# Second attention of a two-layer kernel: scores built from differences of key tiles, a PSUM bank of its own for projected queries, the row maximum transposed later

## The reference, cut to what matters

```python
# second attention: 16 query heads of width 128, 8 key/value heads, 1601 context rows
q = (text_hidden @ Wq).reshape(B, T_text, N_HEADS, HEAD_DIM).transpose(0, 2, 1, 3)
k = (vision_tokens @ Wk).reshape(B, T_vis, N_KV_HEADS, HEAD_DIM).transpose(0, 2, 1, 3)
v = (vision_tokens @ Wv).reshape(B, T_vis, N_KV_HEADS, HEAD_DIM).transpose(0, 2, 1, 3)
scores = jnp.einsum('bhtd,bhsd->bhts', q, k) / scale
scores = jnp.where(mask, scores, -jnp.inf)
attn = jax.nn.softmax(scores, axis=-1)
out = jnp.einsum('bhts,bhsd->bhtd', attn, v)
return out.transpose(0, 2, 1, 3).reshape(B, T_text, N_HEADS * HEAD_DIM) @ Wo
```

## Time and profile before

| | |
|---|---|
| median of 3 runs | 1723.7 us (1720.66 to 1727.66) |
| profiled execution, its own time | 1719.67 us |
| its span, first to last instruction | 1718.4 us |
| mean granted TensorE clock | 0.953 |
| busy: PE, DVE, ACT, POOL | 1520.5, 1257.4, 1056.7, 756.7 us |

### The profile page before, as it was taken

One profiled execution on the slowest core, in us unless ns is written; L12 is line 12 of the kernel. 1 busy time (PEld: TensorE's weight loads), 2 busy tenths in 40 slices (PEclk: granted clock), 3 DMA queues, 4 the chain that ended last, 5 costly groups with the idle time before them and its releaser, 6 DMA issues.

```text
span 1718.4 us, 25847 instructions
## 1 busy us (share of the span) xinstructions
PE 1520.5 (88%) x8715; PEld 747.0 (43%) x8812; DVE 1257.4 (73%) x2460; ACT 1056.7 (61%) x1755; POOL 756.7 (44%) x573
## 2 busy tenths in 40 slices
PE   5787988888878799699999999989999999999989
PEld 3243343343223442234444544444545556455445
DVE  6765766666785346488898789999678886888946
ACT  3567668568657355267766566756457665666734
POOL 3014024024020011166787567676476665566733
PEclk8798999999989799789999999999999999999999
DMA  4001101101120310100001000010000000000000
GB/s 151 1 1 44 36 2 26 34 1 24 37 80 2 161 38 1 29 20 1 20 20 31 1 1 26 1 30 2 1 1 1 1 1 1 1 1 1 1 1 25
DMA packets 20490, 36.72 MB, mean 21 GB/s; under 512 B 4898, under 2 KB 15238, under 8 KB 19334
## 3 DMA queue, kind: packets, MB, share of 16 engines
q1 hardware_dynamic: 20358, 35.07, 7.1%
HBM read 26.53 MB, written 1.15 MB: 16 GB/s over the span
## 4 chain that ended last, share of the span: by engine, by line
PE 43%; DVE 7%; issue 6%; ACT 3%; POOL 1%; DMA 0%; DVEq 0%; POOLq 0%; ACTq 0%
PE BK L510 43%; DVE arena L1678 4%; DVE arena L1701 2%; ACT arena L1780 1%; POOL arena L1817 1%; ACT arena L1784 1%; DVE arena L1670 0%; ACT L1780 0%; ACT L762 0%; PE BK L1601 0%; PE BK L778 0%; DVE arena L1687 0%; ACT arena L1770 0%; DVE arena L1684 0%; DVEq L446 0%
## 5 line engine op out<-in xcount | busy, mean ns | idle before, releaser
L510 PE MATMUL BK<-arena 128*128 128x512 bf16 (+11 forms) x8385 | 1473.7, 374 | 139.3 <-DVE arena L1678 25.1
L510 PEld LDWEIGHTS BK<-arena 128*128 128x128 bf16 (+5 forms) x8482 | 711.5, 114 | 869.3 <-issue 237.2
L1817 POOL TENSOR_TENSOR arena<-arena 128x512 f32<-128x512 f32 (+1 forms) x352 | 504.7, 1434 | 226.8 <-ACT arena L1780 208.7
L1701 DVE TENSOR_TENSOR arena<-arena 128x512 bf16<-128x512 f32 (+1 forms) x416 | 430.3, 1038 | 23.4 <-ACT arena L1784 22.1
L1780 ACT ACTIVATE arena<-BK,arena 128x512 f32<-128x512 f32 (+1 forms) x416 | 285.6, 687 | 255.0 <-PE BK L510 254.5
L1034 DVE TENSOR_REDUCE arena<-BK 128x1 f32<-128x512 f32 x384 | 243.7, 683 | 60.2 <-PE BK L510 59.3
L1678 DVE CUSTOM_DVE_ANT_0 arena<-BK,arena 128x512 bf16<-128x512 f32 x384 | 262.5, 684 | 23.1 <-PE BK L510 5.9
L1184 ACT ACTIVATE arena<-BK 128x512 f32<-128x512 f32 (+1 forms) x416 | 226.0, 598 | 67.2 <-PE BK L510 60.3
L1784 ACT CAST arena<-arena 128x512 bf16<-128x512 f32 (+1 forms) x416 | 257.1, 618 | 13.2
L1224 POOL TENSOR_TENSOR arena<-arena 128x256 f32<-128x256 f32 (+6 forms) x45 | 30.2, 671 | 208.9 <-ACT arena L1123 206.6
L1814 POOL TENSOR_TENSOR arena<-arena 128x512 f32<-128x512 f32 x32 | 45.5, 1422 | 88.7 <-ACT arena L1780 88.7
(11 more groups left out here) (157 smaller groups left out, 825.0 us busy)
## 6 DMA issues: line engine op xcount, KB each, us to landing
arena<-arena SPq DMA_DIRECT2D x144, 50.0 KB, 2.2
arena<-in_ctxT SPq DMA_DIRECT2D x8, 800.5 KB, 5.4
arena<-in_ctxk SPq DMA_DIRECT2D x4, 768.0 KB
arena<-in_wqT SPq DMA_DIRECT2D x1, 2048.0 KB, 8.9
arena<-in_wo SPq DMA_DIRECT2D x1, 2048.0 KB, 13.3
arena<-in_x SPq DMA_DIRECT2D x4, 256.0 KB, 11.3
arena<-in_rsel SPq DMA_DIRECT2D x1, 1024.0 KB, 9.4
arena<-in_rw1T SPq DMA_DIRECT2D x1, 1024.0 KB, 5.1
```

The lines of the kernel that those rows point to most:

```text
L510: return T.matmul(out_, lhsT, rhs, start=start, stop=stop, skip_group_check=True)
L1701: V.tensor_tensor(Pl[k][0:m, :], P1[k][0:m, :], Ph[k][0:m, :], ALU.subtract).then_inc(p_low, 1)
L1817: G.tensor_tensor(acc[0:m, g % 2, :], acc[0:m, g % 2, :], P1[k][0:m, :], ALU.add).then_inc(summed1, 1)
```

## The change

For key tiles 2 to 12 `s1` no longer starts the bank anew. It adds the product of queries with the difference between this tile's keys and those of two tiles earlier, which lie in the same bank; the maximum is already in it. So the fourth matmul is there for tiles 0 and 1 alone. The differences and their bf16 halves (`dch`, and `ctl` from column 256) are formed in stage 1, in `cx`, which now starts at step 12. The projected queries get bank 6, `ql` becomes a piece that comes a tile later on DVE, `o1a` and `o1b` move to bank 7, `o1a` multiplies by one column of ones instead of 128, `m1n` comes a half tile later, and `pace` draws 20 steps for each 26 half tiles.

```diff
@@ stage1: context() is drawn from step 12 on
-            next(cside, None)
+            if s >= E - 4:
+                next(cside, None)
@@ stage2
         def qproj(g):
-            piece("qp", g, bank=7)
-            yield
+            piece("qp", g, bank=6)
+            yield
+            yield
+            piece("ql", g)
             yield
@@ finish
-            piece("o1a", g, bank=6)
+            piece("o1a", g, bank=7)
             yield
             yield
-            piece("o1b", g, bank=6)
+            piece("o1b", g, bank=7)
@@ pace
-            while paced[0] * 26 < (2 * (s + LEAD1) + half) * 18:
+            while paced[0] * 26 < (2 * (s + LEAD1) + half) * 20:
@@ buffers
+        dch = [sb(f"dch{b}", [128, S2 - 256], BF16, L1) for b in range(3)] + [sb("dch3", [128, S2 - 256], BF16, MN)]
-        qa = sb("qa", [128, 1024], F32, L1)
-        qb_ = sb("qb_", [128, 1024], F32, L1)
+        qa = sb("qa", [128, 1024], BF16, L1)
+        qb_ = sb("qb_", [128, 1024], BF16, L1)
@@ vector_moe, cx
                     V.tensor_copy(cth[:, b, :], ctf[b % 2]).then_inc(ct_high, 1)
+                    dve.wait_ge(ct_done, 2 * b + 1)
+                    V.tensor_tensor(ctf[b % 2][:, 0:S2 - 256], ctf[b % 2][:, 256:S2], ctf[b % 2][:, 0:S2 - 256],
+                                    ALU.subtract).then_inc(ct_step, 1)
+                    dve.wait_ge(ct_step, b + 1)
+                    dve.wait_ge(*emptied("fold", H - 1))
+                    V.tensor_copy(dch[b][:, :], ctf[b % 2][:, 0:S2 - 256]).then_inc(ct_step_high, 1)
@@ gpsimd_moe, cx
-                    G.tensor_tensor(ctl[:, b, :], ctf[b % 2], cth[:, b, :], ALU.subtract).then_inc(ct_done, 1)
+                    G.tensor_tensor(ctl[:, b, 0:256], ctf[b % 2][:, 0:256], cth[:, b, 0:256], ALU.subtract).then_inc(ct_done, 1)
+                    pool.wait_ge(ct_step_high, b + 1)
+                    G.tensor_tensor(ctl[:, b, 256:S2], ctf[b % 2][:, 0:S2 - 256], dch[b][:, :],
+                                    ALU.subtract).then_inc(ct_done, 1)
@@ tensor_l1, s1
+                    high = cth[:, b, ks] if kt < 2 else dch[b][:, 128 * kt - 256:128 * kt - 256 + m]
-                    mm(o, cth[:, b, ks], qh[:, r, :], stop=False)
-                    mm(o, cth[:, b, ks], ql[:, r, :], start=False, stop=False)
-                    mm(o, ctl[:, b, ks], qh[:, r, :], start=False, stop=False)
-                    pe.wait_ge(rows1[g % 2], 16 * (g // 2 + 1))
-                    mm(o, onb[:, 0:m], mrw[:, g % 2, :], start=False).then_inc(full[i], 1)
+                    if kt < 2:
+                        pe.wait_ge(rows1[g % 2], 16 * (g // 2 + 1))
+                        mm(o, onb[:, 0:m], mrw[:, g % 2, :], stop=False)
+                    mm(o, high, qh[:, r, :], start=False, stop=False)
+                    mm(o, high, ql[:, r, :], start=False, stop=False)
+                    mm(o, ctl[:, b, ks], qh[:, r, :], start=False).then_inc(full[i], 1)
@@ tensor_l1, o1a
-                        t = mm(BK[6][:, 128 * u:128 * u + 128], acc[:, g % 2, 128 * u:128 * u + 128], ones[:, :])
+                        t = mm(BK[7][:, u:u + 1], acc[:, g % 2, 128 * u:128 * u + 128], ones[:, 0:1])
```

More of the change, by code:

```diff
@@ L610, in program @@
         ckl = sb("ckl", [128, B, NKT, 128], BF16, CK)
+        junk = sb("junk", [128, 512], BF16, CK)
+        dch = [sb(f"dch{b}", [128, S2 - 256], BF16, L1) for b in range(3)] + [sb("dch3", [128, S2 - 256], BF16, MN)]
         mcb = sb("mcb", [128, B, NKT], F32, L1)
@@ L617, in program @@
         ones = sb("ones", [128, 128], F32, L1)
-        onb = sb("onb", [128, 128], BF16, L1)
+        onb = sb("onb", [128, 128], BF16, CT)
         mrw = sb("mrw", [128, 2, 512], BF16, L1)
@@ L622, in program @@
         ql = sb("ql", [128, 3, 512], BF16, L1)
-        junk = sb("junk", [128, 512], BF16, L1)
         mtl = sb("mtl", [128, 4, TAIL], F32, L1)
@@ L642, in program @@
         hs_ = sb("hs_", [128, 3, 2], F32, L1)
-        on1 = sb("on1", [128, 128], F32, L1)
+        on1 = sb("on1", [128, 128], F32, CT)
         F1 = Region(base, 107 * KB)
@@ L1323, in program @@
                              "dn_done", "ct_done", "ct_high"))
+        ct_step, ct_step_high = sem("ct_step"), sem("ct_step_high")
         ac_done = sem("ac_done")
@@ L1560, in sync_moe @@
                     sp.wait_ge(rw_split, 1)
-                    sp.wait_ge(ct_done, b - 1)
+                    sp.wait_ge(ct_done, 2 * b - 2)
                     SP.dma_start(ctf[b % 2], a["ctxT"][b]).then_inc(ld_ctf[b % 2], 16)
@@ L1583, in tensor_l1 @@
                         for dt in range(2):
-                            t = mm(BK[7][:, 256 * j:256 * j + 256], M1[:, dt, 2 * (g % 8) + j, :],
+                            t = mm(BK[6][:, 256 * j:256 * j + 256], M1[:, dt, 2 * (g % 8) + j, :],
                                    xnT[:, dt, S * b:S * b + S], start=(dt == 0), stop=(dt == 1))
-                    t.then_inc(full[7], 1)
+                    t.then_inc(full[6], 1)
                 elif kind == "m1":
@@ L1630, in tensor_l1 @@
                     for u in range(4):
-                        t = mm(BK[6][:, 128 * u:128 * u + 128], acc[:, g % 2, 128 * u:128 * u + 128], ones[:, :])
-                    t.then_inc(full[6], 1)
+                        t = mm(BK[7][:, u:u + 1], acc[:, g % 2, 128 * u:128 * u + 128], ones[:, 0:1])
+                    t.then_inc(full[7], 1)
                 elif kind == "o1b":
@@ L1635, in tensor_l1 @@
                     pe.wait_ge(diag_done, g + 1)
-                    mm(BK[6][:, :], ones[:, :], dg[:, :, :].rearrange("p u n -> p (u n)")).then_inc(full[6], 1)
+                    mm(BK[7][:, :], ones[:, :], dg[:, :, :].rearrange("p u n -> p (u n)")).then_inc(full[7], 1)
                 elif kind == "o1p":
@@ L1660, in vector_l1 @@
                     dve_norm_apply(*arg)
-                elif kind == "qp":
+                elif kind == "ql":
                     g, = arg
-                    dve.wait_ge(full[7], n + 1)
+                    i, n = slot["qp", g]
+                    dve.wait_ge(full[6], n + 1)
                     dve.wait_ge(q_high, g + 1)
-                    V.tensor_tensor(ql[:, g % 3, :], BK[7][:, :], qh[:, g % 3, :], ALU.subtract).then_inc(free[7], 1)
+                    V.tensor_tensor(ql[:, g % 3, :], BK[6][:, :], qh[:, g % 3, :], ALU.subtract).then_inc(free[6], 1)
                 elif kind == "mk":
@@ L1702, in vector_l1 @@
                 elif kind == "o1a":
[L1703 to L1706, removed]
+                    dve.wait_ge(full[7], n + 1)
+                    V.tensor_scalar(dn[:, 0:4], BK[7][:, 0:4], 1e-30, None, ALU.max).then_inc(free[7], 1)
+                    dve.wait_ge(free[7], n + 1)
                     V.reciprocal(dn[:, 4:8], dn[:, 0:4]).then_inc(dn_recip, 1)
@@ L1766, in scalar_l1 @@
                     g, = arg
-                    act.wait_ge(full[7], n + 1)
+                    act.wait_ge(full[6], n + 1)
                     if g >= 3:
                         act.wait_ge(*filled("s1", 13 * (g - 2) - 1))
-                    A.copy(qh[:, g % 3, :], BK[7][:, :]).then_inc(q_high, 1)
+                    A.copy(qh[:, g % 3, :], BK[6][:, :]).then_inc(q_high, 1)
                 elif kind == "s1":
@@ L1786, in scalar_l1 @@
                     g, = arg
-                    act.wait_ge(full[6], n + 1)
+                    act.wait_ge(full[7], n + 1)
                     act.wait_ge(pv_taken, g)
-                    A.copy(rc[:, :], BK[6][:, :]).then_inc(free[6], 1)
+                    A.copy(rc[:, :], BK[7][:, :]).then_inc(free[7], 1)
         def gpsimd_l1():
```

## The result

| | before | after |
|---|---|---|
| median of 8 runs | 1724.4 us | 1743.2 us |
| ratio, 95% interval | | 1.0104 (1.0074 to 1.0134) |
| profiled execution, span | 1719.67, 1718.4 us | 1737.34, 1736.0 us |
| mean granted clock | 0.953 | 0.946 |

The account below looks back on a forecast made before the run. PE was taken to bound light groups, with DVE 1.1 us behind, and mostly DVE the loaded ones. From 1719.7 us, less 23 (light groups) and 16 (loaded), plus 4 (stage 1), came 1685 us; range 1655 to 1716.

Parts of the forecast that it names:

- What bounds the kernel: Stage 2: PE sets the 17 light groups at 25.95 us, DVE's leg 1.1 us behind; DVE mostly sets the 13 loaded ones.
- Fourth matmul, PE's floor of 23.57: `s1` in stage 2: eleven matmuls fewer save PE 2.38 us a group, so its light-group floor falls from 25.95 to 23.57.
- `o1a`: Its fp32 matmuls by one column: weight loads keep the pace, so nothing counted; upper bound 0.9 us a group, 29 in all.
- The loop: `m1n` to `m1n` in light groups: PE's leg 8.67, DVE's 15.43, signal 0.16, together 24.26 us, so DVE becomes the bound.
- `r1` against POOL: DVE's leg in light groups: contention puts the loop at 24.26 to 24.86, taken 24.6; gain 1.35 each, 23 us in all.
- Loaded groups: Thirteen stage 2 groups: DVE's wait at `ql` goes, gaining 1.2 us each (bounds 0 and 2.38), 16 us in all.
- Stage 1: DVE stands in `cx` 3.4 us extra, four times; two are covered, two cost 2 us each: 4 us lost (bounds 0 and 11).
- The rivals: PE keeps the bound, 1652 us (12 of 100); DVE eats most, 1711 (20); slower (8); little effect, within 0.5% (8).
- "Slower": Light groups' `r1` all meet POOL, 1.40 us each: 1762 us; milder cases, 1718 to 1735, likelier; all of it 8 of 100.

Follow-up runs that it names:

- run 4: The kernel before, with POOL adding only 64 of the 512 columns of each tile from the third on: ratio 0.9815, 1696.6 us.
- run 3: The changed kernel, with POOL's additions of tiles 2 to 12 cut to 64 of 512 columns: ratio 0.9518, 1642.8 us.
- run 6: The kernel before, with the fourth matmul of `s1` only for tiles 0 and 1, ahead of the other three, all else unchanged: ratio 1.0070.
- run 1: The kernel before, with the new stage 1 alone (`cx` with differences from step 12, and the buffers), stage 2 as before: ratio 1.0043, 7.4 us over.
- runs 3 to 6: Also takes in the fifth: the changed kernel with POOL's additions of tiles 2 to 12 cut to 256 of 512 columns, ratio 0.9570, 1651.1 us.
- the last kernel: The changed kernel with `cx` spread over three steps and the denominators of the last 6 of 13 tiles on PE: ratio 0.9795, 1691.7 us.

## Why the prediction was wrong, point by point

- **What bounds the kernel: right.** PE set the light groups of before: with POOL cut to an eighth they stay at 25.9 (run 4). DVE was the second, 1.1 us behind.
- **Fourth matmul, PE's floor of 23.57: right**, 23.49 in run 3.
- **`o1a`: right.** The records of one column follow each other at 0.112 us, those of 128 columns did too. The Trainium skill ("TensorE: Matmul & The Clock Gate", LDWEIGHTS) agrees, with 107 ns for a load of 128 columns.
- **The loop: right in form, mis-sized.** PE's leg was 8.27 for 8.67 foretold. DVE's leg was 17.42 for 15.43. The signal took 0.56 for 0.16.
- **"`r1` against POOL": the step that failed.** I bounded its growth from above by the difference between light groups and all groups, 0.085 each, and took half. Start to start the seven `r1` took 0.89, 1.55, 1.06, 1.20, 1.07, 0.60 and 0.60, together 6.97 us for 5.39: 1.00 each, growth 0.23, nearly three times the upper bound. The other error was 0.89 us of DVE waiting for PE ahead of the second maximum (1552.89), where `o1b` and the `v1` of the tile stand on PE; against it, the rest of the leg was 0.5 shorter. The loop comes to 26.26, and light groups lose 0.3 instead of gaining 1.35. The bound was wrong because it treated the meeting of the two engines as a matter of how full POOL is (67% or 71%). It is one of when: an `r1` that starts during an addition ends 0.55 us after it, one that starts first is not slowed. Run 6 shows the same POOL work, the same instructions on DVE, and 1.6 us more, only because the exponentials come earlier. The whole contention hung on a bound that was about to be removed.
- **Loaded groups: wrong.** Foretold 16 us of gain, mostly from the wait at `ql`. The wait went, and DVE's time was filled by longer `r1`: the 15 slowest groups sum up to 468.2 us for 472.4, the other 15 lose 4.8. All 30 are at 864.3 for 863.7.
- **Stage 1: mechanism right, size off.** Difference 1.56 (foretold 1.8), cast 0.87 (0.83), POOL and the hops 0.75 (0.8): 3.2 each time. I had counted two of four as covered, 4 us; run 1 gives 7.4 with both stage 1 and its buffers. At the second `cx` PE ran dry, and its granted clock fell: 680 to 690 us is busy 4.40 us with a mean granted clock of 0.71, so partly at the 1.2 GHz level, against 1.00 between 640 and 650, where it was busy 9.95. The fourth `cx` stood in the stage's end, which I had taken for cover.
- **The rivals.** What came is the milder case of "Slower", 1718 to 1735, a little beyond: its mechanism is shown by runs 3 to 6. Its deciding point was 1.08 us for `r1` in the leg by the prediction's terms; the 1.00 start to start (1.08 in the rows' own durations, which overlap by 0.08) with the wait of 0.89 passes it. I gave it 8 of 100 on the argument that the maxima shift DVE away from POOL. They don't: in the windows of four light groups 32 of 52 `r1` start during one of POOL's operations before, with 0.58 us of it left on average, and after the change 38 of 52, with 0.80 left. The Trainium skill ("GPSIMD Engine Reference", Specifications) names the shared interfaces and DVE's two SBUF inputs; the runs agree (`r1` has two and is held up, the maximum has one and stays at 0.68), and between the changed kernel and run 3 lie 5.9% of the time.

What stays open: the 3.4 us behind the last `m1n`. From there to the last `r1` it is 42.1 us for 39.6, and 34.0 in run 3, so most of it probably is the same contention in the last group; the rest I did not find.

## What to carry to other kernels

When an engine that sets the pace is relieved, everything behind it comes earlier, and operations of DVE and POOL that share operands' interfaces and start from the same event begin to coincide; look at how much of the second engine's time is short only because the first one was late, and price the relief with the contended duration, not with the mean of today: for each operation ask whether it will start while the other engine's is running, and add what will be left of that. A test that shrinks the other party (here POOL's columns) tells in one run whether a saving is unreal or merely masked. Then move the contending work to the engine that was relieved: the matmuls saved here paid only after some of POOL's additions had been put in their place.

## What the runs showed of the hardware

- `r1` (128x512, two inputs in SBUF) on DVE: 0.684 us on average and never above 0.69 in the 77 instances of the kernel before that met no operation of POOL; up to 1.81 us in light groups of the changed kernel where they met. The one that starts second pays: an `r1` that starts during POOL's operation ends 0.55 us after it (261 instances in before), one that starts first stays at 0.68 (78). POOL's addition is 1.27 alone, and 1.53 as the median of those in before that started while an `r1` was running and met no second one. DVE's maximum, with one input in PSUM, stays at 0.68 beside POOL (245 that start during an addition, none above 0.70).
- Matmuls with bf16 weights of 128x128 and one moving column followed each other at 0.025 us in the last kernel, where I had estimated 0.056; fp32 ones at 0.112. Column sums on PE from bf16 halves cost 0.2 us a tile, against 1.27 to 1.5 on POOL.
